# Row numbers a group ahead, an earlier first pass, and columns loaded by the round

## The reference

```
x = layernorm(x + L0(x))      x = layernorm(x + L1(x))
L0: w = relu(edge_feat @ W1 + b1) @ W2 + b2          (4 paths of 8x8 per edge)
    message = 8x8 products of w with the source node's scalars and vectors,
              turned by the edge's spherical harmonics; summed by destination;
              plus a self term x @ si
L1: R = relu(distance * w1 + b1) @ w2 + b2           (paths between l = 0 and l = 1)
    message = R times spherical harmonics of the edge's direction times the
              source node's features; summed by destination
```

## Time and profile before

| | |
|---|---|
| median of three executions | 4051.86 us |
| profiled execution, its own time | 4059.36 us |
| its span | 4057.4 us |
| PE matmul busy | 3377.3 us (83%) |
| DVE busy | 3460.9 us (85%) |
| ACT busy | 2184.8 us (54%) |
| POOL busy | 2953.0 us (73%) |
| mean granted PE clock | 0.908 of full speed |

### The profile page before, as it was taken

The page is one execution under the profiler, slowest core; times in us unless marked ns, Lnnn a source line. Parts: engine busy times, 40 slices in busy tenths (PEclk is TensorE's granted clock), DMA queues, the critical chain, the costliest instruction groups (busy, mean ns, idle before and its releaser), DMA issues. The chain is left out here.

```text
span 4057.4 us, 95500 instructions
## 1 busy us (share of the span) xinstructions
PE 3377.3 (83%) x23156; PEld 1945.7 (48%) x23156; DVE 3460.9 (85%) x5277; ACT 2184.8 (54%) x6587; POOL 2953.0 (73%) x3087
## 2 busy tenths in 40 slices
PE   4777777777777777777559999999999999999996
PEld 3444444444444444444335555555555555555553
DVE  8888888888888888888759999889889888988887
ACT  3555555555555555555335565555555555555554
POOL 5777777777777777777377777777777777777772
PEclk7888888888888888888779999999999999999998
DMA  3111111111111111111212222222221222222221
GB/s 107 35 33 32 34 32 33 34 33 35 32 33 32 33 32 34 36 32 33 35 38 48 45 44 44 44 44 44 47 45 41 47 44 44 44 43 44 44 44 28
DMA packets 238827, 162.68 MB, mean 40 GB/s; under 512 B 143937, under 2 KB 212594, under 8 KB 238066
## 3 DMA queue, kind: packets, MB, share of 16 engines
q1 hardware_dynamic: 104338, 91.78, 8.7%
q0 software_dynamic: 98560, 50.66, 8.6%
q10 hardware_dynamic: 35650, 17.88, 1.7%
HBM read 148.83 MB, written 10.43 MB: 39 GB/s over the span
## 5 line engine op out<-in xcount | busy, mean ns | idle before, releaser
L430 POOL DMA_INDIRECT rows<-x_rows,src x1540 | 1483.2, 963 | 536.6 <-issue 526.6
L430 POOL DMA_INDIRECT rows<-in_x,src x1540 | 1468.9, 954 | 485.6 <-issue 472.3
L775 PE MATMUL red<-prod,ident 128*128 128x336 f32 (+1 forms) x4704 | 1511.2, 475 | 1.4 <-DVE prod L1073 1.2
L775 PEld LDWEIGHTS red<-prod,ident 128*128 128x128 f32 x4704 | 892.3, 195 | 635.4 <-issue 193.3
L1073 DVE TENSOR_TENSOR prod<-wps,arena 128x896 f32<-128x896 f32 x782 | 832.4, 1083 | 176.2 <-PE wps L762 159.0
L755 PE MATMUL wps<-bias_parts,ones 64*128 64x448 bf16 (+1 forms) x2346 | 471.4, 398 | 610.7 <-DVE prod L1067 452.4
L565 ACT ACTIVATE gap<-iota,slot_plan 128x128 bf16<-128x128 f32 x3136 | 935.6, 386 | 7.0
L762 PE MATMUL wps<-w_sb,hidden 64*128 64x448 f32 (+1 forms) x3920 | 746.9, 476 | 0.0
L583 ACT ACTIVATE arena<-red 128x336 f32<-128x336 f32 (+1 forms) x294 | 135.5, 461 | 1103.5 <-PE red L775 1102.9
L755 PEld LDWEIGHTS wps<-bias_parts,ones 64*128 64x128 bf16 x2346 | 114.6, 94 | 1135.3 <-DVE prod L1067 562.4
L1082 DVE TENSOR_REDUCE arena<-prod 128x384 f32<-128x3072 f32 (+1 forms) x195 | 520.9, 2671 | 0.1
(11 more groups left out here) (127 smaller groups left out, 3025.3 us busy)
## 6 DMA issues: line engine op xcount, KB each, us to landing
mlp<-in_dist SPq DMA_DIRECT2D x196, 256.0 KB
fetched<-in_x SPq DMA_DIRECT2D x3072, 0.1 KB
fetched<-x_rows SPq DMA_DIRECT2D x3072, 0.1 KB
mlp<-in_feat SPq DMA_DIRECT2D x98, 256.0 KB
rows<-in_x,src POOLq DMA_INDIRECT x1540
rows<-x_rows,src POOLq DMA_INDIRECT x1540
frames<-frame ACTq DMA_DIRECT2D x49, 144.0 KB
geo<-frames ACTq DMA_DIRECT2D x98, 72.0 KB
```

What stands on the lines that cost most here:

```text
L430: nc.gpsimd.indirect_dma_start(out=rows[z][:, t, :], out_offset=None, in_=table_rows, in_offset=bass.IndirectOffsetOnAxis(ap=src_sb[z][:, ...
L775: ins = nc.tensor.matmul(red[:, bank * 512:bank * 512 + cols], ident[:], pr[:, i, :, a:b, :], start=(i == 0), stop=(i == MUL - 1))
```

## The change

- Row numbers: `src` is laid out by groups of four chunks (and one group of padding). SP loads 64 numbers per partition in one transfer for the group after the current one, ahead of that group's last 32 fetches; POOL waits once per group. Each of the two buffers holds one group, so POOL's and SP's loops take two groups per turn.
- First pass: SP and POOL no longer wait for the number of passes before layer 0. Their loop bodies run at least once in any case; they read the number into a register at the end of the first pass.
- Set-up: the two iotas come with the identity from DRAM as one constant; the all-reduce becomes a matmul against the identity and a reduction on DVE; the constant loads move from SP's queue to ACT's, the initial counts to PE; the edge-place computation takes 3 passes over the data instead of 8; the weights of layer 1 are prepared between the layers (`prepare_second`); `measure` moves behind the edge places.
- Frames: those of the last round are made between the layers instead of at the head of layer 0's last round, and ACT stores them there.
- Columns: DVE loads the eight columns of a round at the head of the round in one call, instead of four at the head of each chunk's body; for the last chunks 12 in one call instead of three calls. The last whole round stands outside of the loop.
- Last chunk of layer 1: its 12 tiles are summed 8 by PE and 4 by DVE; before, all 12 by PE.

```diff
+FETCH_PAIRS = FETCHES // 2
+SRC_GROUPS = FETCHES + 1
...
+LAST_PE_SUMS = (((0, 8),), ((0, 6), (6, 8)))
+LAST_PE_TILES = 8
...
+        consts = sb("consts", [P, 2 * P + 1])
+        ident, iota, iota_p = consts[:, 0:P], consts[:, P:2 * P], consts[:, 2 * P:2 * P + 1]
...
-        src_sb = slots(lambda z: sb(f"src{z}", [P, TILES], I32))
+        src_sb = slots(lambda b: sb(f"src{b}", [P, FETCH_CHUNKS * TILES], I32))
...
+        def read_passes(eng, register):
+
+            eng.wait_ge(windows_known, 1)
+            eng.reg_load(register, passes_i[0:1, 0:1])
+
+        def src_loads(eng, j, pair, b):
+
+            return eng.snap(j * (FETCH_PAIRS + 1 - b) + (pair + 1))
...
+            def load_source(n, b, group):
+
+                sp.dma_start(src_sb[b][:], src[bass.ds(group, 1)].rearrange("g p t -> p (g t)")
+                             ).then_inc(layers[n].src_loaded[b], 16)
...
                             load_mlp(n, z, r, k)
+                            if m == FETCH_CHUNKS - 1:
+                                sp.wait_ge(s.rows_read[RING - 1], r0)
+                                load_source(n, 1 - b, h + 1)
...
+                    for z in range(RING):
+                        sp.wait_ge(s.rows_read[z], round_of(sp, j, 0))
+                    load_source(n, 0, 0)
+                    with sp.Fori(0, FETCH_PAIRS) as pair:
+                        group(pair * 2, 0)
+                        group(pair * 2 + 1, 1)
...
+                    if n == 0:
+                        read_passes(sp, count)
+
+            stream(0, sp.alloc_register("sp_passes"))
...
-            nc.gpsimd.iota(iota[:], pattern=[[1, P]], base=0, channel_multiplier=0,
-                           allow_small_or_imprecise_dtypes=True)
-            nc.gpsimd.iota(iota_p[:], pattern=[[0, 1]], base=0, channel_multiplier=1,
-                           allow_small_or_imprecise_dtypes=True).then_inc(iota_ready, 1)
-
-            pool.wait_ge(spans_reduced, 1)
-            nc.gpsimd.partition_all_reduce(span_max[:, 1:2], span_max[:, 0:1], P,
-                                           bass.bass_isa.ReduceOp.max).then_inc(spans_known, 1)
-
-            def gather(n, z, r, tiles=TILES):
+            def gather(n, z, r, m, b, loads, tiles=TILES):
 
                 s = layers[n]
                 pool.wait_ge(s.rows_read[z], r)
                 pool.wait_ge(s.rows_copied[z], r)
-                pool.wait_ge(s.src_loaded[z], r * 16 + 16)
+                if m == 0:
+                    pool.wait_ge(s.src_loaded[b], loads * 16)
...
+            gather_all(0, pool.alloc_register("pool_passes"))
             count = passes(pool)
-            gather_all(0, count)
             pool.wait_ge(x1_stored, len(PIECES) * 16)
             gather_all(1, count)
...
+            act.dma_start(w1_sb[:], w1_0).then_inc(loaded["weights"], 16)
+            act.dma_start(b1_sb[:, 0:1], b1_0).then_inc(loaded["weights"], 16)
+            act.dma_start(w2_sb[0][:], w2_0).then_inc(loaded["weights"], 16)
+            act.dma_start(consts[:], constants).then_inc(loaded["weights"], 16)
+            act.dma_start(xs, x_self).then_inc(loaded["self"], 16)
+            act.dma_start(si_sb[:], si).then_inc(loaded["self"], 16)
+            act.dma_start(table[:, 0:BLOCKS, :], x_nodes).then_inc(loaded["nodes"], 16)
+            act.dma_start(rel_sb[:], rel).then_inc(loaded["rel"], 16)
+            act.dma_start(dst_t[:], dst).then_inc(loaded["dst"], 16)
+            act.dma_start(w1c_sb[:], w1_1).then_inc(loaded["l1_weights"], 16)
+            act.dma_start(b1_sb[:, 1:2], b1_1).then_inc(loaded["l1_weights"], 16)
+            act.dma_start(w2_sb[1][:], w2_1).then_inc(loaded["l1_weights"], 16)
+            spread_windows()
             square_lengths()
-            spread_windows()
+            read_windows()
...
+            act.wait_ge(loaded["l1_weights"], 48)
+            store_frames(ROUNDS - 1, act.snap(count * FRAME_ROUNDS + 1))
+            act.wait_ge(frames_stored, act.snap(count * (16 * FRAME_ROUNDS) + 32))
...
+            pe.wait_ge(loaded["weights"], 64)
+            pe.wait_ge(spans_reduced, 1)
+            nc.tensor.matmul(hps[:, 0:P], span_max[:, 0:1].broadcast_to([P, P]), ident, start=True, stop=True
+                             ).then_inc(spans_known, 1)
...
+            chain(nc.vector.tensor_reduce(span_max[:, 1:2], hps[:, 0:P], AX_X, ALU.max))
             chain(nc.vector.tensor_scalar(fits[:], span_max[:, 1:2], float(P) - 0.5, None, ALU.is_lt))
             chain(nc.vector.tensor_scalar(passes_f[:], fits[:], float(1 - PASSES_ALL), float(PASSES_ALL),
                                           ALU.mult, ALU.add))
             st.done(nc.vector.tensor_copy(passes_i[:], passes_f[:]))
+            st.done(nc.vector.tensor_scalar(low_bits[:], fits[:], float(P), -1.0, ALU.mult, ALU.add))
...
+            st.done(nc.vector.tensor_scalar(negkey0, by_chunk(dst_t[:]), 0.0, FAR, ALU.is_lt, ALU.mult))
+            chain(nc.vector.tensor_tensor(low, dst_t[:], low_bits[:].broadcast_to([P, CHUNKS * TILES]), ALU.bitwise_and))
+            st.done(nc.vector.tensor_tensor(negkey0, negkey0, by_chunk(low), ALU.subtract))
+            measure()
...
-            def load_columns(k):
+            def load_columns(k, chunks):
 
                 _, cols = nc.values_load_multi_w_load_instructions(
-                    offs[0:1, bass.ds(k * GROUPS, GROUPS)], engines=(mybir.EngineType.DVE,), min_val=0,
+                    offs[0:1, bass.ds(k * GROUPS, chunks * GROUPS)], engines=(mybir.EngineType.DVE,), min_val=0,
                     max_val=(BLOCKS - 1) * FEAT)
-                return cols
-
-            def body0(i, z, r, st, last, tail, cols):
+                return [cols[c * GROUPS:(c + 1) * GROUPS] for c in range(chunks)]
...
+                    def whole_round(i):
                         r = round_of(dve, j, i)
+                        cols = load_columns(i * RING, RING)
                         for z in range(RING):
                             st = Steps(dve, s.dve_body, j * (bodies * BODY_STEPS[n])
                                        + i * (RING * BODY_STEPS[n]) + (z + 1) * BODY_STEPS[n])
-                            body(n, i, z, r, st, False, False, load_columns(i * RING + z))
+                            body(n, i, z, r, st, False, False, cols[z],
+                                 dve.snap(j * FRAME_ROUNDS + (i + 1)))
                             assert st.n == BODY_STEPS[n], ("body", n, st.n)
+
+                    with dve.Fori(0, ROUNDS - 2) as i:
+                        whole_round(i)
+                    whole_round(ROUNDS - 2)
...
+            make_frames(ROUNDS - 1, dve.snap(count * FRAME_ROUNDS + 1))
+            prepare_second()
...
```

More of the change, by code:

```diff
@@ L609, in body @@
                         distances(n, z1, r1, 0, steps)
-                    if n == 0 and z == 1:
-                        store_frames(i, r)
+                    if n == 0 and z == 1 and not last:
+                        store_frames(i, frames_of)
                     if not last:
@@ L1163, in body0 @@
                 sm, sm_v = sums_of(0, z, 0), sums_of(0, z, 1)
-                if z == 0:
-                    make_frames(i, r, Steps(dve, frame_steps, (r - 1) * FRAME_STEPS))
+                if z == 0 and not last:
+                    make_frames(i, frames_of)
                 if not tail:
@@ L1252, in body1 @@
                 if not tail:
-                    multiply(1, z1, r1, 5)
+                    multiply(1, z1, r1, 5, last)
                 cut_rest(1, z, r)
@@ L1258, in body1 @@
                     projected = project(1, i + 1, z, r + 1, st)
+                elif not tail:
+                    sum_tiles(1, z1, r1, st, last)
                 add_window(3, cols, z1, st)
@@ L1350, in scale_nodes, with prepare_second @@
                                         ).then_inc(nodes_ready, 1)
+            def prepare_second():
+                dve.wait_ge(loaded["l1_weights"], 48)
+                w2 = w2_sb[1]
+                for path, factor in ((3, K_11_2), (0, K_00), (1, K_01), (2, K_10), (6, K_11_1)):
+                    st.done(nc.vector.tensor_scalar(w2[:, :, path, :], w2[:, :, path, :], factor, None, ALU.mult))
+                st.need(st.n)
+                chain(nc.vector.tensor_scalar(w2_tmp[:], w2[:, :, 3, :], -1.0 / 3.0, None, ALU.mult))
+                chain(nc.vector.scalar_tensor_tensor(out=w2[:, :, 4, :], in0=w2[:, :, 4, :], scalar=K_11_0, in1=w2_tmp[:],
+                                                     op0=ALU.mult, op1=ALU.add))
+                st.done(nc.vector.tensor_tensor(w2[:, :, 3, :], w2[:, :, 3, :], w2[:, :, 4, :], ALU.add))
+                chain(nc.vector.tensor_tensor(w2[:, :, 5, :], w2[:, :, 4, :], w2[:, :, 6, :], ALU.add))
+                chain(nc.vector.tensor_tensor(w2[:, :, 4, :], w2[:, :, 4, :], w2[:, :, 6, :], ALU.subtract))
+                split_bias(1)
             def normalize(n):
```

169 lines of the change are left out of this document (65 added, 104 removed).

## The result

The changed kernel takes 4092.32 us (median of four executions, 4088.31 to 4093.09) against 4052.33 us before (four, 4048.19 to 4052.96): slower by 40 us, ratio 1.0098 with a 95% interval of 1.0086 to 1.011. The direction was forecast; the size (+11.9 us, range up to 4083) was not. Read n of a layer stands for DVE's read of chunk n's gathered rows.

What follows compares the result with a forecast made beforehand. POOL's gathers were taken to bound layer 0, and POOL and DVE to lie about 1.0 us in 40 apart in layer 1. Terms: -17.8 - 4.0 + 1.0 + 34.9 - 2.2 = +11.9, so 4063.8 us; range 4024 to 4083.

Steps and rivals of the forecast that it cites:

- start, to gather 33: Set-up and first 32 gathers: gather 1 at 8.5 us and gather 33 at 55.4 instead of 73.2, -17.8 us.
- layer 0, gather 33 to read 96: Layer 0's rounds: later columns only shrink DVE's 3.2 us waits for rows, POOL keeps the pace, so nothing.
- last frames, read 96 to 97: Head of layer 0's last round: DVE no longer works on frames there, -4.0 us.
- between the layers, to read 2: POOL's first gathers of layer 1 slowed by DVE copies, +1.0 us; plus 1.5 for round 0 ahead of read 2.
- layer 1, read 2 to read 96: 47 rounds of layer 1 at 40.55 us, 1905.9 us against 1872.5, as DVE becomes slower than POOL.
- last chunk, read 96 to the end: End of layer 1: PE sums fewer tiles, so DVE's 4.35 us wait shrinks against a 2.01 us reduction, -2.2 us.
- row numbers by the group: POOL's row numbers: no wait in steady state, worth nothing; 2.4 us only if POOL stays layer 1's bound.
- columns, +34.9 us: Round heads in layer 1: eight values expose 1.49 us per round, putting DVE's round at 40.55 us above POOL's 40.05.
- the frames' count: Round head on DVE's sequencer: one more register instruction, 0.07 us of the 1.49 exposed per round.
- the clock: Rival B, layer 1: PE's longer pause halves its clock every round, 48 x 1.29 = 62 us, 4126 us; chance 0.09.
- the margin: Layer 1: DVE's own pace needs 1835.8 us against 1872.5 measured, 36.6 us in all before added DVE time costs.
- rival A: Layer 1: the column head stays hidden and POOL remains the bound, -25.4 us, 4026.5 us; chance 0.20.

## Why the prediction was wrong in size

Measured are the differences of the two shown profiles (4059.36 and 4088.31 us) and of the two second ones (4050.64 and 4092.24 us), which lie near the medians.

| step | forecast | first profiles | second profiles |
|---|---|---|---|
| start, to gather 33 | -17.8 | -18.0 | -18.4 |
| layer 0, gather 33 to read 96 | 0 | +2.2 | +9.6 |
| last frames, read 96 to 97 | -4.0 | -4.2 | -3.7 |
| between the layers, to read 2 | +1.0, +1.5 for round 0 | +1.3 | +1.3 |
| layer 1, read 2 to read 96 | +33.4 | +51.4 | +56.7 |
| last chunk, read 96 to the end | -2.2 | -3.6 | -3.8 |
| sum | +11.9 | +29.1 | +41.7 |

The row numbers by the group were forecast at nothing (2.4 us where POOL is the bound); taken back they made +2.9 us, not told from 0.

The mechanism was right: cover for four values was just used up, the second body gave nothing back, DVE passed POOL, and POOL waits for its reads. The step that failed is the size of the term **columns, +34.9 us**. Taken back alone it gave 59.6 us. It was too small in three places.

First, 1.49 per round was 1.60: 47 x 0.11 = 5.2 us. Load and values were right within 0.03 (1.39 measured alone); what I priced at 0.07 for the frames' count, with all that stands ahead of the load, was 0.21.

Second, the clock. I made it a rival that either comes in every round at 1.29 us or not at all, and wrote against it that the new pause is half of the one at 4006.18. Half the pause gave the dip in a third of the rounds: 51.4 - 33.4 - 5.2 leaves 12.8 us, and 14 bodies of 0.91 us are 12.7. This is the largest part. A rival that can come in part belongs in the forecast's own range: a third of its 62 us, 21 us, on top of the range's 4083 would have taken in the result. That the part would be a third could not be read from the rows.

Third, the margin. I took POOL's pace from one profile, 1872.5 us between reads 2 and 96; the second profile of the kernel before has 1867.3. The margin was 31.5 us (1867.3 - 1835.8) and not 36.6, which makes the change 5.2 us dearer. The shown profile was 7.5 us above the median in part because of this stretch, and once DVE is the bound that part is no longer in the time; carrying all terms over to the plain runs unchanged was the mistake.

The three add up to the second profiles: 33.4 + 5.2 + 12.8 + 5.2 = 56.6 of 56.7 us.

A fourth miss is outside of the columns: layer 0 was priced at nothing and took 2.2 us more in one pair of profiles and 9.6 in the other. With the 5.2 of the margin this is where the 11 us lie that the first two profiles don't show. Whether the change causes it is not shown. From gather 33 to the last gather of layer 0 the two profiles of before took 1894 and 1898 us, nine with the early start 1898 to 1914 (without the kernel of twelve values), but two without it, the kernel before with eight values and the changed one without the early start, 1903 and 1910. Three quarters of the spread are in the gathers' own durations (1428 to 1443 us in sum); what lengthens them stays open. It is also why the kernel with the columns by the chunk, rival A made real, took 4032.7 and not 4026.5: its gathers took 1907 us.

In layer 0 the waits for rows, 3.2 us a round in the earlier trace rows, did not shrink, they are gone. DVE's waits from 500 to 1500 us, at the frames' head, before and after:

```profile
DVE frame_tmp L991 <- issue: 49.8, 26, 1.9
```

```profile
DVE frame_tmp L1003 <- issue: 82.7, 25, 3.3
```

The head takes 1.3 us a round more for the sequencer, and new waits for PE and ACT (36.8 us in the 1000) take most of the rest. So the changed kernel had next to no slack in layer 0.

One row was misread. The prediction took the first gather's 1.32 us instead of 0.95 as agreeing with a copy, cast or tensor_scalar of DVE that holds the port pair. Beside that gather (26.35 to 27.67) DVE ran tensor_tensor and scalar_tensor_tensor operations. What the traces show of this stands at the end.

## What to carry to other kernels

Register loads with bounds cost DVE's sequencer a fixed time per value here, and they were free only as far as the reduce that ran ahead of them covered them: halving the calls saves nothing if it puts twice the values under the same cover. Where two engines are 1 us in 40 apart, price every edit of the slower-looking one per round, and take the margin between the bounds from more than one profile, since here only one of the two paces varied. And a pause of PE that is half of one that cost clock may cost it some of the time: put a part of it into the sum.

## What the runs showed of the hardware

How often the granted clock fell in layer 1 went with PE's own pause behind the head of a round (from the end of one matmul to the start of the next). With 0.77 us (six values, DVE idle 1.27) it stayed at 1.00 in all 47 rounds. With 1.14 (the kernel before with eight values, DVE idle 1.65) it fell to 0.50 in 15 of 47, with 1.36 (the changed kernel, 1.86) in 14 of 47 and at the same bodies in two executions, with 2.61 (twelve values, 3.11) in every round. It is not only this head: the kernel before fell twice in layer 1, and once in its second profile, each time behind a pause of 1.07 us, of which it had 13 and 10. Equal pauses fell on both sides, and what decides between them is open. The cost of a dip did not follow the pause either: 0.91 us a body behind 1.36, some 1.6 behind 1.14.

DVE's sequencer takes 0.28 us to hold one value to its bounds, and loads 4, 8 or 12 values in 0.34, 0.60 or 0.85 us (median over the loads of one line).

An indirect gather of 0.95 us took up to 2.83 us in the set-up, and which ones were slow goes with what DVE ran beside them. The slowest of the changed kernel, and DVE's tensor_tensor on two operands in SBUF beside it:

```profile
11.65 2.83 POOL L427 DMA_INDIRECT rows<-in_x,src  x1 [0.30 <-issue]
```

```profile
11.38 2.29 DVE L904 TENSOR_TENSOR arena<-arena 98x2048 f32<-98x2048 f32 x1
```

It ended 0.81 us behind the end of the tensor_tensor. Beside copies and tensor_scalars of DVE at 38 us a gather took 2.39 us, in the kernel with the weights prepared in the set-up too, where the same work comes at 52 us. Gathers that started beside a reduce of DVE (2.29 us at 13.70, 3.85 at 31.71) took 0.94 or 0.95 us.
